# Inversion stopped at 64x64 blocks, the right-hand side solved by two blocks

## The reference

```python
def step(S, inp):
    q_t, k_t, v_t, g_t, b_t = inp
    S = S * jnp.exp(g_t)[..., None, None]
    u = (v_t - jnp.einsum('bhk,bhkv->bhv', k_t, S)) * b_t[..., None]
    S = S + jnp.einsum('bhk,bhv->bhkv', k_t, u)
    o_t = jnp.einsum('bhk,bhkv->bhv', q_t, S)
    return (S, o_t)
...
h = _layernorm(x, axis=-1) * (1 + ca) + sa
x = x + ga * _L0_attn_ref(h, ...)
h = _layernorm(x, axis=-1) * (1 + cb) + sb
x = x + gb * _L0_ffn_ref(h, ...)
...
x = x + ga * _L1_attn_ref(h, ...)
...
x = x + gb * _L1_ffn_ref(h, ...)
```

## Time and profile before

| | us |
|---|---|
| median of 3 runs (3083.61 to 3086.35) | 3085.35 |
| the profiled execution | 3073.01 |
| its span, first to last instruction | 3071.2 |
| PE busy | 2502.6 (81%) |
| DVE busy | 2245.6 (73%) |
| ACT busy | 1247.8 (41%) |
| POOL busy | 641.2 (21%) |

### The profile page before, as it was taken

The page is one execution under the profiler, slowest core; times in us unless marked ns, Lnnn a source line. Parts: engine busy times, 40 slices in busy tenths (PEclk is TensorE's granted clock), DMA queues, the critical chain, the costliest instruction groups (busy, mean ns, idle before and its releaser), DMA issues.

```text
span 3071.2 us, 61542 instructions
## 1 busy us (share of the span) xinstructions
PE 2502.6 (81%) x22808; PEld 2004.1 (65%) x22808; DVE 2245.6 (73%) x5056; ACT 1247.8 (41%) x2761; POOL 641.2 (21%) x528
## 2 busy tenths in 40 slices
PE   2477978879887887978889797887988788897897
PEld 1166766757766576766757676575766657676686
DVE  1668777787877778787687877778787777877762
ACT  0233533435344253533425353243534424353342
POOL 0222122131212222122131212313121122202210
PEclk9869989989899898989989998998989989898998
DMA  4000000000000000000000000000000000000000
GB/s 119 2 2 3 2 8 3 7 3 7 2 3 8 2 7 3 6 2 3 7 3 7 2 3 8 3 7 3 7 2 3 7 3 7 3 4 5 1 5 2
DMA packets 24718, 21.52 MB, mean 7 GB/s; under 512 B 7210, under 2 KB 21443, under 8 KB 24403
## 3 DMA queue, kind: packets, MB, share of 16 engines
q1 hardware_dynamic: 24402, 17.14, 2.0%
HBM read 15.00 MB, written 2.13 MB: 6 GB/s over the span
## 4 chain that ended last, share of the span: by engine, by line
PE 60%; DVE 18%; issue 13%; POOL 4%; ACT 3%; SPq 1%; DMA 1%; DVEq 0%; POOLq 0%; ACTq 0%
PE banks L984 8%; PE banks L1160 8%; PE banks L1150 8%; PE banks L1034 6%; PE banks L918 4%; PE banks L927 3%; DVE wide L1332 3%; PE banks L976 3%; DVE wide L1344 2%; PE banks L855 2%; PE banks L962 2%; PE banks L1019 2%; PE banks L1026 2%; PE banks L897 2%; POOL lg L536 2%
## 5 line engine op out<-in xcount | busy, mean ns | idle before, releaser
L532 POOL TENSOR_TENSOR wide<-wide 128x512 f32<-128x512 f32 x128 | 243.5, 1902 | 872.5 <-DVE wide L1352 560.7
L1461 DVE SCALAR_TENSOR_TENSOR wide<-pad,conv,wide 128x256 f32<-128x256 f32 x864 | 389.1, 518 | 0.0
L984 PE MATMUL banks<-inv,mats 64*64 64x64 f32 x5120 | 198.0, 237 | 141.8 <-DVE inv L1505 104.6
L1344 DVE TENSOR_TENSOR_SCAN wide<-wide 128x1024 f32<-128x1024 f32 x128 | 308.4, 2409 | 1.9 <-ACT wide L634 0.3
L634 ACT ACTIVATE wide<-small,a_neg 128x255 f32<-128x255 f32 x512 | 217.8, 497 | 201.8 <-DVE wide L1344 198.9
L984 PEld LDWEIGHTS banks<-inv,mats 64*64 64x64 f32 x5120 | 185.2, 152 | 160.1 <-issue 159.2
L1150 PE MATMUL banks<-inv,up 128*128 128x256 f32 x1024 | 264.9, 387 | 0.0
L1160 PE MATMUL banks<-down,inv 128*128 128x128 f32 x2048 | 257.7, 277 | 0.0
L768 ACT ACTIVATE inv<-banks,up1b 128x256 f32<-128x256 f32 x512 | 215.0, 481 | 105.0 <-PE banks L1150 104.8
L1160 PEld LDWEIGHTS banks<-down,inv 128*128 128x128 f32 x2048 | 249.9, 192 | 5.8
L984 PE MATMUL banks<-inv 64*64 64x64 f32 x5120 | 189.0, 233 | 29.0 <-DVE inv L1513 28.9
(11 more groups left out here) (281 smaller groups left out, 5160.1 us busy)
## 6 DMA issues: line engine op xcount, KB each, us to landing
gates_bc<-gate_rows SPq DMA_DIRECT2D x32, 128.0 KB, 2.9
up<-in_W SPq DMA_DIRECT2D x1, 2048.0 KB
x<-in_x SPq DMA_DIRECT2D x16, 128.0 KB, 2.1
out<-xn_y SPq DMA_DIRECT2D x16, 128.0 KB, 1.9
wide<-in_wmod SPq DMA_DIRECT2D x2, 384.0 KB
con<-in_con SPq DMA_DIRECT2D x1, 724.0 KB
w_k<-in_Wk SPq DMA_DIRECT2D x1, 512.0 KB
w_q<-in_Wq SPq DMA_DIRECT2D x1, 512.0 KB
```

Source lines behind the costliest of these rows:

```text
L532: g.tensor_tensor(ypart[p % 2], r[:, 0:512], r[:, 512:1024], ALU.add).then_inc(a_yp.h, 1)
L984: last = t.matmul(PS[a:b, out, h * HALF:(h + 1) * HALF], weights(h, a, b), values(h, a, b), start=True, stop=True)
L1344: v.tensor_tensor_scan(state[st % 2], decay[st % 2], drive[st % 2], 0.0, ALU.mult, ALU.add).then_inc(a_h.h, 1)
L1461: v.scalar_tensor_tensor(dst, src, w, dst, ALU.mult, ALU.add).then_inc(c_conv.h, 1)
```

## The change

`LEVELS` ends at 32, so the inversion stops with the two diagonal 64x64 blocks, A (upper) and B (lower), in the tile `TTd`. The tile `TTf` and the path of the last level go. The apply stage solves by two blocks: `c_top` on PE multiplies the upper half of R by A (8 products of 64x64 weights and 32 columns), ACT copies the result to SBUF, `c_low` on PE multiplies it by the lower left block of M, DVE adds that to the lower half of R, and `c_X` on PE multiplies the sum by B. `c_low` and `c_X` call `keep_warm` first, and so does `c_top` of channel 1. The strings of `TURNS` for PE, DVE and ACT are new; POOL's is the same. `lev_T` has no step on PE and ACT any more.

```diff
-LEVELS = [2, 4, 8, 16, 32, 64]
+LEVELS = [2, 4, 8, 16, 32]
...
-APPLY = [("c_R", 0), ("c_X", 0), ("c_U", 0), ("c_O", 0), ("c_S",), ("c_o", 0), ("c_kS",), ("c_R", 1), ("c_X", 1),
+APPLY = [("c_R", 0), ("c_top", 0), ("c_low", 0), ("c_X", 0), ("c_U", 0), ("c_O", 0), ("c_S",), ("c_o", 0), ("c_kS",), ("c_R", 1), ("c_top", 1), ("c_low", 1), ("c_X", 1),
...
-        TTf = sb("TTf", [P, TILES, NH, P])
+        top_x = inv[0:HALF, 6, 256:512].rearrange("p (h v) -> p h v", v=DV)
...
-            g.memset(TTf[:], 0.0)
...
             def lev_TT(i, l, ch):
-                if l + 2 < NL:
+                if l + 1 < NL:
                     s.wait_ge(c_T.h, c_T.at(i, (l + 1) * TILES + ch + 1))
                 else:
                     s.wait_ge(c_TTp.h, c_TTp.at(i, l * TILES + ch + 1))
...
+                s.copy(TTd[ch].rearrange("p h t -> p (h t)"), bank(5 + ch)).then_inc(c_TT.h, 1)
+
+            def c_top(i, ch):
+                s.wait_ge(c_tp.h, c_tp.at(i, ch + 1))
+                s.copy(top_x.rearrange("p h v -> p (h v)"), PS[0:HALF, 3 + ch, 0:256]).then_inc(c_tx.h, 1)
...
-            def c_X_(i, ch):
+            def c_top(i, ch):
                 if ch == 1:
                     keep_warm(4)
                 if ch == 0:
                     t.wait_ge(c_R0.h, c_R0.at(i, 1))
-                    t.wait_ge(c_TT.h, c_TT.at(i, NL * TILES))
+                    t.wait_ge(c_TT.h, c_TT.at(i, (NL - 1) * TILES + 1))
                 else:
                     t.wait_ge(c_R1.h, c_R1.at(i, 3))
-                per_head(3 + ch, lambda h: TTf[:, ch, h, :], R).then_inc(c_X.h, 1)
+                    t.wait_ge(c_TT.h, c_TT.at(i, NL * TILES))
+                t.sem_inc(released, 1)
+                for h in range(NH):
+                    last = t.matmul(PS[0:HALF, 3 + ch, h * DV:(h + 1) * DV], TTd[ch][0:HALF, h, :], R[0:HALF, h, :], start=True, stop=True)
+                last.then_inc(c_tp.h, 1)
+
+            def c_low_(i, ch):
+                keep_warm(7 - ch)
+                t.wait_ge(c_tx.h, c_tx.at(i, ch + 1))
+                t.sem_inc(released, 1)
+                for h in range(NH):
+                    last = t.matmul(PS[HALF:P, 3 + ch, 256 + h * DV:256 + (h + 1) * DV], MTc[ch][0:HALF, h, HALF:P], top_x[:, h, :],
+                                    start=True, stop=True)
+                last.then_inc(c_lp.h, 1)
+
+            def c_X_(i, ch):
+                keep_warm(7 - ch)
+                t.wait_ge(c_low.h, c_low.at(i, ch + 1))
+                t.sem_inc(released, 1)
+                for h in range(NH):
+                    last = t.matmul(PS[HALF:P, 3 + ch, h * DV:(h + 1) * DV], TTd[ch][HALF:P, h, :], R[HALF:P, h, :], start=True, stop=True)
+                last.then_inc(c_X.h, 1)
...
+            def c_low_(i, ch):
+                v.wait_ge(c_lp.h, c_lp.at(i, ch + 1))
...
+                v.tensor_tensor(R[HALF:P], R[HALF:P], PS[HALF:P, 3 + ch, 256:512].rearrange("p (h v) -> p h v", v=DV),
+                                ALU.add).then_inc(c_low.h, 1)
```

More of the change, by code:

```diff
@@ L71, in constants @@
     c[:, C_MASK2:C_MASK2 + HALF] = fold(((col % 2 == 1) & (row == col - 1)) | (row == col))
-    for n, s in enumerate(LEVELS[:-1]):
+    for n, s in enumerate(LEVELS):
         low = (row // (2 * s) == col // (2 * s)) & (row // s % 2 == 1) & (col // s % 2 == 0)
@@ L1014, in lev_TT @@
                 t.sem_inc(released, 1)
-                if l + 2 < NL or l + 2 == NL:
-                    last = halves(5 + ch, lambda h, a, b: WW[ch][a:b, h, :], lambda h, a, b: TTd[ch][a:b, h, :])
-                else:
-                    for h in range(NH):
-                        last = t.matmul(PS[0:HALF, 5 + ch, h * HALF:(h + 1) * HALF], WW[ch][HALF:P, h, :], TTf[HALF:P, ch, h, HALF:P],
-                                        start=True, stop=True)
-                last.then_inc(c_TTp.h, 1)
+                halves(5 + ch, lambda h, a, b: WW[ch][a:b, h, :], lambda h, a, b: TTd[ch][a:b, h, :]).then_inc(c_TTp.h, 1)
             def keep_warm(bk):
```

70 lines of the change are left out of this document (22 added, 48 removed).

## The result

The changed kernel takes 3111.5 us (median of 4 runs, 3108.6 to 3115.5) against 3085.4 (4 runs): a ratio of 1.0086, 95% interval 1.0069 to 1.0104. It is 0.9% slower. The forecast was 3034 in a range of 2985 to 3080; the result lies outside, on the other side of no change.

The account below looks back on a forecast made before the run. It took DVE as the bound in the scan, PE in the last 62.60 us, no engine in front. Terms of -3.26 a pass, -48.9 over fifteen, and -2.5 behind the loop total -51.4: median 3034, range 2985 to 3080.

Parts of the forecast that it names:

- Router and attention, -1.3: Behind the scan, probabilities times values leaves the chain behind the expert sums on PE: -1.3 us a pass, ends -2.0 and +0.6.
- In the last part ... nothing.: In the pass's last part the same PE work is only dealt out differently and PE was full: no change.
- first scan: Front stretch: the first scan starts earlier, with level 4 no longer ahead of the step: -4.9 us a pass, ends -4.5 and -5.6.
- level 4, copies, additions, late scan, waits, to the reduction: Scan stretch on DVE: level 4 +2.7, copies -1.3, additions +0.84, one 3.35 us scan shortened -0.5, waits for PE's solve +1.2.
- Behind the loop: Where y runs alone after the loop: first U gains 4.7 us, channel 1's solve loses 2.2, together -2.5.
- rival 1: Slower: the solve's three dependent PE groups between scans run at 1.2 GHz, +46 us, about 3131; chance 0.13.
- Rival 2: Nothing: DVE was full anyway and x's own chain holds the first scan in place, -9 us, 3076; chance 0.12.
- Rival 4: Tile-shape changes on PE cost: ten a pass at 0.2 us each, leaving -18 us, 3067; chance 0.05.
- Rival 3: More: every term at its good end and the clock kind to most passes, 2970 to 2990 us; chance 0.10.

Follow-up runs that it names:

- e2: The changed kernel with two more pairs of fillers on PE ahead of its wait for the router's coefficients; ratio 1.0077 to the kernel before.
- e4: The kernel before with the changed kernel's order behind the scan alone, its own inversion, solve and scan kept; ratio 1.0173 to the kernel before.
- e1: The changed kernel with the residual of y's experts moved back ahead of the last state products on DVE; ratio 1.0061 to the kernel before.
- e13: The changed kernel with the old order from the scan's end to the pass's end, new inversion, solve and scan kept; ratio 0.9978 to the kernel before.
- e8: The changed kernel with level 4 of the inversion put back ahead of the first scan; ratio 1.0232 to the kernel before.
- e11: e9 with level 4 of the inversion put back ahead of the first scan; ratio 1.0163 to the kernel before.
- e14: e13 plus eleven pairs of fillers a pass, at the pass's start and behind the scan, none ahead of the coefficients; 3043.6 us, ratio 0.9879.
- e7: The kernel before plus thirteen pairs of fillers a pass, six at its start, two of the others ahead of the router's coefficients; ratio 1.0020.
- e12: The kernel before plus fillers in its own waits, six pairs at the pass's start, four ahead of y's second normalisation's transposes, none ahead of the coefficients; ratio 1.0019.
- e3: The changed kernel with the router and attention steps back in the old order on PE, DVE and ACT; ratio 1.0128 to the kernel before.
- e9: The changed kernel with e1's move and the fillers of e7, but five pairs ahead of the router's coefficients; ratio 1.0079 to the kernel before.

## Why the prediction was wrong

**The step that failed is "Router and attention, -1.3"**, with its worse end of +0.6. Its mechanism was right: the product of probabilities and values left the chain behind the sums, and from the sums to y's first expert product it is 6.1 instead of 7.7, -1.6. What it left out is the clock in the stretch ahead. PE's full stretch does not begin when x's coefficients are there but when PE has done x's expert products, and most of those ran at 1.2 GHz: +4.3 to the sums. The prediction priced that clock only inside the solve. Moving the scores ahead took from PE the work that had stood between its first expert products, left it a wait of 2.21, and in the measured pass the granted clock behind that wait was 0.60 (8.89 became 12.71). e2 showed the price within one execution, e4 that the order behind the scan brings it without the new solve. That the wait itself brought the clock down is not shown: in e2 it was 0.72 behind a wait of 0.3 and 1.00 behind one of 1.3.

**The second miss is "In the last part ... nothing."** For PE it holds: 62.1 after 62.3, in nearly every run. But DVE's order moved there too, and the residual at its end holds back the next pass: +1.4 (e1).

The other terms, each as the stage table has it:

| term | forecast | measured |
|---|---|---|
| first scan | -4.9 | -4.3 |
| level 4, copies, additions, late scan, waits, to the reduction | +2.9 | +2.7 |
| to the sums and to y's expert product | -1.3 | +4.3 - 1.6 = +2.7 |
| last part | 0 | -0.2 + 1.4 = +1.2 |
| sum | -3.3 | +2.3 |
| behind the loop | -2.5 | -1.7 |

The first two held in the changed kernel. With the old order behind the scan (e13) the two together are -3.6 + 3.5 instead of -4.3 + 2.7, so the low clock takes from them too when it falls there, which the prediction did not price either. Their details can be read on DVE between the first scan and the reduction:

```profile
1559.18 1.30 DVE L1497 STREAM_TRANSPOSE inv<-banks 128x512 f32<-128x512 f32 x2
...
1563.80 1.40 DVE L1501 TENSOR_TENSOR inv<-banks,con 128x512 f32<-128x512 f32 x2
...
1570.22 0.42 DVE L1530 TENSOR_TENSOR inv<-inv,banks 64x256 f32<-64x256 f32 x1 [0.25 <-PE banks L1023]
...
1597.53 0.42 DVE L1552 TENSOR_TENSOR inv<-banks,inv 128x256 f32<-128x256 f32 x1 [1.33 <-PE banks L1001]
```

Level 4 costs 2.7 there, an addition 0.42; DVE waits 0.25 for the lower product, in channel 1 as in channel 0. The longest wait is 1.33, for the output product of channel 1, not for the solve. No scan is late: 2275, 2283 and 2353 ns are the least, the median and the most of all 128. On PE the solve of channel 0:

```profile
1567.01 1.07 PE L1015 MATMUL banks<-inv 64*64 64x32 f32 x16
...
1568.98 1.12 PE L1023 MATMUL banks<-inv,mats 64*64 64x32 f32 x16
...
1570.80 1.09 PE L1032 MATMUL banks<-inv 64*64 64x32 f32 x16 [0.16 <-DVE inv L1530]
```

A group of 32 columns costs the 1.09 that the prediction took, at a granted clock of 1.00. So rival 1, the cold solve, did not happen; only its direction, slower, came true. Rival 2 fell with the first scan. Rival 4: of all PE instructions in this pass one has idle time of no shown cause, 0.34 at a change from 96 to 64 rows; so ten changes at 0.2 are not seen. The drain of which the Trainium skill speaks (TensorEngine Tiling (Array Packing), Tiling Modes) has no length here beyond that. Rival 3 did not occur either. No rival named the low clock behind the scan.

**Behind the loop** y's first U comes 6.7 behind the second level-4 merge instead of 11.2 (2980.99 to 2992.17 before), and its second U 5.8 behind the right-hand side instead of 3.1: 4.5 won and 2.7 lost (3.1 was 3000.01 to 3003.15), beside a forecast of 4.7 and 2.2.

```profile
3018.38 0.69 DVE L1501 TENSOR_TENSOR inv<-banks,con 128x512 f32<-128x512 f32 x1 [0.25 <-PE banks L975]
...
3025.11 0.42 DVE L1537 TENSOR_TENSOR inv<-banks,cU 128x256 f32<-128x256 f32 x1 [1.27 <-PE banks L1032]
...
3032.95 0.43 DVE L1522 TENSOR_TENSOR inv<-inv 128x256 f32<-128x256 f32 x1
...
3038.75 0.42 DVE L1537 TENSOR_TENSOR inv<-banks,cU 128x256 f32<-128x256 f32 x1 [1.27 <-PE banks L1032]
```

**What is shown and what is open.** Shown: the loss lies behind the scan (e4), in two places (stages of e1, e2, e4), and the greater one is the granted clock (two kinds of passes in e2 with the same instructions). Shown too: level 4 inside the scan is a gain (e8; e11 agrees, but for its late start). The new inversion, solve and scan are worth 0.2% with the old order behind the scan (e13) and 1.2% with fillers (e14), where nearly the same fillers gave the kernel before nothing (e7, e12). Open: what decides, pass by pass, where the low clock falls. In e3 it went partly into the full stretch, in e13 partly into the scan, in e12 behind the coefficients when the part ahead was filled; these were read from the granted clock after the fact, and none of the theories here forecast them. Open as well: what sets PE's late start in e9 and e11.

## What to carry to other kernels

When an order changes, list for PE not only its work but its waits: the products behind a new wait ran at half the clock here, and where such products stand on the path that begins the next full stretch, price them at that clock before counting a gain. Do not count on fillers to remove the low clock: in e12 they only moved it. Look at what stands last in the loop body on the engine that begins the next pass; here 1.1 us of work moved there came back in full at that point. And judge a change of about 1% with fillers on both sides as well as without: the new inversion, solve and scan were worth 0.2% without (e13) and about 1.4% with them (0.9879 of e14 beside 1.0020 of e7, whose fillers are nearly the same).
